# A linear attention loop in software pipeline: the gates' and queries' projections open TensorE's step, both turnings back follow

## The reference

```python
q = hidden_states @ Wq;  k = hidden_states @ Wk;  v = hidden_states @ Wv
beta = jax.nn.sigmoid(hidden_states @ Wb + bb)
gate = silu(hidden_states @ Wg)
q = silu(causal_dwconv(q, qconv_w, qconv_b))      # 4 taps along the tokens
k = silu(causal_dwconv(k, kconv_w, kconv_b))
q = layernorm(q.reshape(Bs, Ls, H, DK), qn_w, qn_b)
k = layernorm(k.reshape(Bs, Ls, H, DK), kn_w, kn_b)
...
    S = (1.0 - b) * S + b * (v_t[..., :, None] * k_t[..., None, :])
    o_t = jnp.einsum('bhvk,bhk->bhv', S, q_t)
...
o = o * gate
return o @ Wo
```

## Time and profile before

| what | us |
|---|---|
| median of 3 runs | 1209.75 (1208.91 to 1213.49) |
| the profiled execution, its own time | 1208.93 |
| its span in the profile | 1207.1 |
| TensorE busy | 1134.1 (94% of the span) |
| VectorE busy | 922.7 (76%) |
| ScalarE busy | 772.3 (64%) |
| GpSimd busy | 634.9 (53%) |
| first projection of linear attention starts at | 362.85 |
| last residual addition of linear attention starts at | 1153.57 |

### The profile page before, as it was taken

The page is one execution under the profiler, slowest core; times in us unless marked ns, Lnnn a source line. Parts: engine busy times, 40 slices in busy tenths (PEclk is TensorE's granted clock), DMA queues, the critical chain, the costliest instruction groups (busy, mean ns, idle before and its releaser), DMA issues. The chain is left out here.

```text
span 1207.1 us, 22452 instructions
## 1 busy us (share of the span) xinstructions
PE 1134.1 (94%) x7558; PEld 910.6 (75%) x7558; DVE 922.7 (76%) x2124; ACT 772.3 (64%) x1533; POOL 634.9 (53%) x1078
## 2 busy tenths in 40 slices
PE   8999999886977899999999999999999999999768
PEld 7443434326646799999999999999999999999646
DVE  6788887836446788888888888888888888888452
ACT  3377676762435777676777777676777677776324
POOL 4020400000703686777787686777687777767520
PEclk9899999987899999999999999999999999999989
DMA  6434334402102101111201211110211111111020
GB/s 171 54 54 55 54 54 55 54 2 76 47 8 67 46 32 63 50 47 32 81 32 47 78 35 47 67 47 32 81 32 47 67 47 37 42 47 33 16 70 1
DMA packets 23449, 60.50 MB, mean 50 GB/s; under 512 B 3367, under 2 KB 8359, under 8 KB 22183
## 3 DMA queue, kind: packets, MB, share of 16 engines
q1 hardware_dynamic: 23335, 59.07, 18.8%
HBM read 44.67 MB, written 2.33 MB: 39 GB/s over the span
## 5 line engine op out<-in xcount | busy, mean ns | idle before, releaser
L1665 DVE SCALAR_TENSOR_TENSOR l_conv<-l_proj_q,par,l_conv 128x511 f32<-128x511 f32 (+2 forms) x192 | 142.4, 742 | 113.1 <-ACT l_conv L1581 110.8
L690 DVE TENSOR_REDUCE a_neg_max<-a_scores 128x1 f32<-128x512 f32 x244 | 155.0, 682 | 36.6 <-PE a_scores L418 34.8
L609 ACT ACTIVATE a_probs<-a_scores_t 128x512 f32<-128x512 f32 x256 | 138.4, 600 | 62.8 <-PE a_scores_t L437 61.8
L1407 POOL TENSOR_TENSOR l_k_tok<-l_normed,k_norm 128x384 f32<-128x384 f32 x64 | 65.0, 1015 | 157.8 <-ACT l_normed L1598 157.8
L1665 DVE SCALAR_TENSOR_TENSOR l_conv<-l_proj_k,par,l_conv 128x511 f32<-128x511 f32 (+2 forms) x192 | 142.8, 744 | 4.6
L1587 ACT ACTIVATE l_conv<-l_conv,par 128x512 f32<-128x512 f32 x128 | 92.5, 723 | 77.4 <-DVE l_conv L1665 74.5
L1598 ACT ACTIVATE l_normed<-l_turn_q,l_shift,l_scale 128x128 f32<-128x128 f32 x256 | 96.3, 457 | 26.0 <-POOL l_shift L1399 25.8
L1397 POOL TENSOR_TENSOR l_scale<-l_small,l_minus_half 128x8 f32<-128x8 f32 x64 | 105.1, 1642 | 5.0
L1598 ACT ACTIVATE l_normed<-l_turn_k,l_shift,l_scale 128x128 f32<-128x128 f32 x256 | 97.1, 481 | 0.0
L1541 PE MATMUL l_outp<-l_masked,l_values 128*128 128x128 f32 x512 | 88.7, 275 | 0.9 <-DVE x_tok L1693 0.9
L1640 ACT ACTIVATE l_gate<-l_proj_gv 128x512 f32<-128x512 f32 x64 | 38.2, 597 | 79.8 <-PE l_proj_gv L1463 79.8
(11 more groups left out here) (329 smaller groups left out, 3546.8 us busy)
## 6 DMA issues: line engine op xcount, KB each, us to landing
l_keep<-keep_rows SPq DMA_DIRECT2D x64, 448.0 KB, 3.5
a_stack<-a_dense SPq DMA_DIRECT2D x90, 128.0 KB, 5.0
head_raw<-w_heads SPq DMA_DIRECT2D x8, 1024.0 KB, 6.7
x_tok<-x SPq DMA_DIRECT2D x4, 512.0 KB, 8.2
wo_raw<-w_o SPq DMA_DIRECT2D x1, 2048.0 KB, 10.5
out<-x_tok SPq DMA_DIRECT2D x1, 1920.0 KB
a_stack<-a_max_rows_t SPq DMA_DIRECT2D x64, 4.0 KB
ctx_tok<-w_qkv SPq DMA_DIRECT2D x1, 768.0 KB, 6.7
```

The source lines that it names most:

```text
L609: act.activation(probs[:, n % 2, h, :], scores_t[(4 * n + h) % TURNS][:], ACT.Exp, scale=SOFT_SCALE).then_inc(probs_done, 1)
L690: dve.tensor_reduce(neg_max[:, g % 2, at:at + 1], max_bank(g, j), AX.X, ALU.max, negate=True).then_inc(max_done, 1)
L1665: ins = dve.scalar_tensor_tensor(conv[:, w, m, s:], proj[w][:, 0:SEQ - s], par[:, h, tap:tap + 1], conv[:, w, m, s:], ALU.mult, ALU.add)
```

## The change

Each engine gets another order inside a step; no computation is added, removed or resized.

- TensorE: the step opens with the gates' and the queries' projections. Then come both turnings back, the keys' projection, both turnings to tokens, and the rest as before. Since the projection out ends the step before, the gates' projection now stands right behind it.
- VectorE: `gated` moves between the second and third later tap of the keys; `values` comes directly behind the third; `masked` and `carry` come behind `values`.
- ScalarE: the first tap of the queries comes before the affine of the queries; both affines stand together. `gated_high` moves behind the copy of the chunk state, and works on unit u-3 instead of u-4.
- GpSimd: the late queries come behind the keys' three operations; `gated_low` comes behind `scales` and works on unit u-3 instead of u-4.

```diff
@@ gpsimd step @@
                 if has(u, 2):
-                    late_rows(u - 2, (k - 2) % BODY, keep_count(pair, k, 2))
+                    late_keys(u - 2)
                     decayed(u - 2, (k - 2) % BODY)
-                if has(u, 4):
-                    gated_low(u - 4, (k - 4) % BODY)
+                    late_queries(u - 2, (k - 2) % BODY, keep_count(pair, k, 2))
                 if has(u, 1):
                     scales(u - 1, (k - 1) % BODY)
+                if has(u, 3):
+                    gated_low(u - 3, (k - 3) % BODY)
@@ tensor step @@
-                for w in range(2):
-                    if has(u, 2):
+                if has(u, 0):
+                    if k == 0:
+                        wait(pe, w_ready, 4 * pair)
+                    wait(pe, values_done, u)
+                    project(proj_gv, G, k, of).then_inc(g_proj, 1)
+                    wait(pe, conv_sem[Q], u)
+                    project(proj_q, Q, k, of).then_inc(q_proj, 1)
+                if has(u, 2):
+                    for w in range(2):
                         turn_back(u - 2, w)
-                    if has(u, 0):
-                        if k == 0 and w == 0:
-                            wait(pe, w_ready, 4 * pair)
-                        wait(pe, conv_sem[w], u)
-                        project(proj[w], w, k, of).then_inc(proj_sem[w], 1)
+                if has(u, 0):
+                    wait(pe, conv_sem[K], u)
+                    project(proj_k, K, k, of).then_inc(k_proj, 1)
                 if has(u, 1):
                     for w in range(2):
                         turn_tokens(u - 1, (k - 1) % BODY, w)
-                if has(u, 0):
-                    wait(pe, values_done, u)
-                    project(proj_gv, G, k, of).then_inc(g_proj, 1)
@@ scalar step @@
-                if has(u, 2):
-                    norm_affine(u - 2, (k - 2) % BODY, 0)
-                if has(u, 4):
-                    gated_high(u - 4, (k - 4) % BODY)
                 if has(u, 0):
                     tap(pair, k, u, 0)
                 if has(u, 2):
+                    norm_affine(u - 2, (k - 2) % BODY, 0)
                     norm_affine(u - 2, (k - 2) % BODY, 1)
...
                     act.activation(state[:, k % 2, 0, :], chunks[:, 0:DK], ACT.Copy).then_inc(state_copied, 1)
+                if has(u, 3):
+                    gated_high(u - 3, (k - 3) % BODY)
                 if has(u, 0):
                     silu(pair, k, u, 1)
@@ vector step @@
                     convolve(pair, k, u, 1, 2)
-                    convolve(pair, k, u, 1, 3)
-                if has(u, 2):
-                    (masked of unit u-2)
                 if has(u, 3):
                     (gated of unit u-3)
-                if has(u, 2):
-                    carry(u - 2, k)
                 if has(u, 0):
+                    convolve(pair, k, u, 1, 3)
                     (values of unit u)
+                if has(u, 2):
+                    (masked of unit u-2)
+                if has(u, 2):
+                    carry(u - 2, k)
```

More of the change, by code:

```diff
@@ L1399, in scales, with late_queries, late_keys @@
                 pool.tensor_tensor(shift[:, i, :], small[:, 5, :], scale[:, i, :], ALU.mult).then_inc(scales_ready, 1)
-            def late_rows(v, k, rows_in):
+            def late_queries(v, k, rows_in):
                 m = k % 2
+                wait(pool, keep_loaded[m], rows_in)
+                wait(pool, qk_ready[0], v + 1)
+                wait(pool, read_out, v - 1)
+                pool.tensor_tensor(q_late[:, m, :], qk[:, 0, m, P:], keep[:, m, SEQ:],
+                                   ALU.mult).then_inc(q_decayed, 1)
+            def late_keys(v):
                 wide = [P, LATER, DK]
@@ L1408, in late_rows @@
                                    k_norm[:, 0, :].unsqueeze(1).to_broadcast(wide), ALU.mult).then_inc(k_scaled, 1)
[L1409 to L1413, removed]
                 wait(pool, k_scaled, v + 1)
@@ L1734, in step @@
                         ALU.mult).then_inc(values_done, 1)
+                if has(u, 2):
+                    v = u - 2
+                    wait(dve, decay_done, v + 1)
+                    wait(dve, read_out, v - 1)
+                    wait(dve, scored, v + 1)
+                    dve.tensor_tensor(masked[:, k % 2, :], scores[:], decay[:], ALU.mult).then_inc(masked_done, 1)
+                if has(u, 2):
+                    carry(u - 2, k)
                 if has(u, 1):
```

## The result

The changed kernel took 1212.99 us, median of 16 runs (1208.17 to 1216.88), beside 1208.8 us for the kernel before in 16 runs (1203.96 to 1213.57): a ratio of 1.0032, 95% interval 1.0016 to 1.0048. The same two kernels were compared twice more among the experiments, with 12 runs of the changed one each: 0.9990 (0.9969 to 1.0011) and 1.0013 (0.9993 to 1.0032). Weighted by the inverse squares of their intervals the three give about 1.0015: some 2 us slower, under the 6 us that were named as what can be told. The first two intervals don't overlap, so an interval holds the scatter inside one comparison and not what changes from one comparison to the next.

The account below looks back on a forecast made before the run. TensorE's own stream was taken as the bound, 11.87 us a step. Merging -0.4, first steps +0.4 and last steps -0.7 gave -0.7 us: 1208.2 on the profile's scale, 1209.0 as median, range 1206 to 1214.

Parts of the forecast that it names:

- TensorE's stream sets the pace of the steady part: Steady linear attention steps: TensorE's pieces add up to 11.87 us a step with nothing left over, before and after.
- Rival (c): TensorE's stream: two fewer changes between turnings and projections a step save 10 us, giving 1199; chance 0.04.
- rival (d): Steady step: TensorE could run faster, the norm loop sets 11.87; loosened, 18 us are saved, giving 1191; chance 0.03.
- One merge saves 0.006 us: TensorE: joining neighbouring turnings saves 0.006 us, one counted a step over 59 steps: 0.4 us, 1.2 at most.
- the 0.17 us of cover: Old order: the queries' norm ends 0.23 us before its turning back starts, less 0.06 of hand-off.
- The values' chain ends at 11.44 with 0.26 us of cover: Steady step: VectorE's values end at 11.44 us, before the next gates' projection at 11.87; cost zero.
- rival (b): Steady step: the values' chain exceeds 11.70 us to its hand-off and TensorE waits; 1215 to 1223; chance 0.15.
- Masking, carry and scan come behind the values and end at 2.1 of the next step: VectorE, steady step: they end at about 14.0 us, before their readers need them; cost zero.
- The first steps cost between -0.3 and +1.1, taken at +0.4: First steps: 0.3 us won at full TensorE clock, against half of an estimated 1.4 us for slower clock.
- the half clock: First steps: TensorE again at 1.2 GHz for six matmuls and a turning, estimated 1.4 us; half of it taken.
- The last steps save 0.7: End: the queries' multiply no longer stands between the keys' two GpSimd steps; -0.7 us, between 0 and -0.8.
- The sum was -0.7: Whole kernel: merging -0.4, first steps +0.4, last steps -0.7 us; together -0.7.

Follow-up runs that it names:

- the filled kernel: Changed kernel with 26 additional matmuls, results never read, where TensorE waits in its first two steps; ratio 1.0007 (0.9989 to 1.0025).

## Why the prediction was wrong

The measured 1212.99 us lies inside the range of 1206 to 1214, but the forecast was 0.7 us faster, and the first comparison is slower beyond its interval. Pooled it is 0.15%, within the 0.5% that got a chance of 0.81. By its own steps:

- *TensorE's stream sets the pace of the steady part, and the new order does not change that.* Right. 11.888 us a step in three profiles, forecast 11.87. Rival (c), 10 us by fewer changes of kind, is excluded by it, and rival (d), a pace under 11.8, too.
- *One merge saves 0.006 us.* Wrong in sign, and without weight: the stream got 0.015 us longer. A projection that follows another takes 1.40 us for its six; a turning and a projection took 1.829 together in the old order, 1.393 for the projection if four turnings are 0.436. Against the first profile this is +0.8 instead of -0.4 us. But the old order's own step is 11.89 in two of three profiles, since its norm chain is just as long; the 0.17 us of cover that one step showed was not there in every execution.
- *The values' chain ends at 11.44 with 0.26 us of cover.* Right: 11.50 in a step with the stretched scan, no wait. This is rival (b), and it did not happen.
- *Masking, carry and scan come behind the values and end at 2.1 of the next step; none costs anything.* Right in the time, wrong in the trace. The scan ends at 812.33 + 3.22 - 811.57 = 3.98 in half the steps, as it now meets GpSimd's weight operation and, held by it, the next one. I followed the order of the waits and took every duration from rows in which another engine was idle beside it. The changed kernel's cover held; the old order's does not.
- *The first steps cost between -0.3 and +1.1, taken at +0.4.* This is the step that failed, and in it the price of the half clock. The first steps cost 2.0 to 2.8 us. The chain of waits was right at full clock: from the third gates' projection on I had steps of 11.0, 11.5 and 11.6 us, the filled kernel has 11.01 and twice 11.5, and its sixth chunks come at 87.18 against 87.63 before, 0.45 earlier, where I had 0.3. The half clock I priced at 1.4 us, from the old place, where six matmuls and a turning stood on the chain, and took half of that. In the old kernel it does cost about as much, 1.6 us in the one step that it falls on (13.14 against 11.59, 13.07 against 11.46). In the changed kernel it costs twice that, 2.8 to 2.9 us: in the first profile on the twelve projections and the first turnings right behind the longest wait, in the other two on the third step and again on the fourth. All of these stand on the chain. Why the new first steps get twice as much of the half clock is not shown.
- *The last steps save 0.7.* Right in mechanism: the last chunks start 21.4 us behind the sixty-second unit's, instead of 22.2 to 22.3. In all, 38.3 to 38.5 us stand against 38.8 to 39.9, so 0.4 to 1.6; at like clock it is 0.4 to 0.5.

The sum was -0.7 and the profiles show +1.4 on the mean (+0.2 to +3.0 from pair to pair). The 4 us of the first comparison are more than that. Two further comparisons did not repeat them, so I take them as chance; that is argued and not shown. What is shown is how large such chance can be. Outside linear attention, where the code is the same, the profiled executions of the two kernels took 412.3 to 417.1 us. And the time of a whole execution goes with its mean granted clock: in the third comparison the runs of the kernel before took about 1207 us at 0.976, 1211 at 0.972 and 1215 at 0.969.

## What to carry to other kernels

When a software pipeline is bound by one engine's stream, a new order inside its steps is worth what it does to the filling and draining steps: look there for which work stands on the chain behind the long waits, since it can run at half clock (two steps of 11.01 and 11.54 us took 25.3 to 25.5 in all). Give the first steps their own order if another is better for them (0.9991 here by itself, 0.9956 with filled waits). And when an instruction is moved, list what runs beside it on the other engines at the new place, because its duration can depend on them (1.36 against 3.2 us for the scan here).

## What the runs showed of the hardware

- Four VectorE scans of 128 columns from SBUF to SBUF take 1.36 us alone and 3.2 where they meet GpSimd's 128x512 float32 subtract and its next multiply: one under way when such an operation runs adds 1.1 to 1.4 us instead of 0.32. VectorE's operations with an input in PSUM keep their time beside a GpSimd subtract of the same form (the masking 0.68 us, the carry 0.34 each). GpSimd's subtract goes from 1.28 us (812.57, behind the scan) to 1.45 and 1.48 (beside it).
- TensorE ran at 1.2 GHz again in the first steps, and not at the same place in each execution of one program. Old order: behind waits of 2.35 and 2.37 us in the first two profiles, with full clock behind the 3.30 us wait of the step before, and the other way round in the third (3.33 and 2.38 us). Changed kernel: behind 3.07 us alone in one profile, and behind that wait and again in the step behind 1.84 us in two. Additional matmuls in the waits kept it at 2.4 GHz (0.49 us for the first projection instead of 0.79). In the old order such matmuls in the first two steps did not help, since the fall came behind the wait of 2.35 us in the fourth.
- The execution in which a profile falls changes the old kernel's step from 11.873 to 11.89 us at the same granted clock of 1.00.
